# Placing the uses of one shared PSUM bank among the score tiles of an attention stage

## The reference, cut to what matters

```python
x = x + 0.5 * ffn(layernorm(x))        # 8 experts, top 2, and a shared one
x = x + attention(layernorm(x))        # 16 heads of 64, latents of 128
x = x + 0.5 * ffn(layernorm(x))        # x is (8, 1024, 256)

def attention(x):
    h = layernorm(x) * ln_scale + ln_bias
    c_q, c_kv = h @ w_down_q.T, h @ w_down_kv.T        # latents
    q, k, v = (c_q @ w_up_q.T, c_kv @ w_up_k.T, c_kv @ w_up_v.T)   # per head
    q, k = rope(q), rope(k)
    p = softmax(q @ k.T / 8)
    return (p @ v) @ w_out.T + x
```

## Time and profile before

| | |
|---|---|
| median of 3 runs | 4113.1 us (4110.75 to 4115.69) |
| profiled execution: its time | 4111.56 us |
| its span, first to last instruction | 4109.6 us |
| PE busy | 3897.7 us, 95% |
| POOL / DVE / ACT busy | 2948.8 / 2856.5 / 2535.5 us |
| mean granted TensorE clock | 0.987 |

### The profile page before, as it was taken

One profiled execution on the slowest core, in us unless ns is written; L12 is line 12 of the kernel. 1 busy time (PEld: TensorE's weight loads), 2 busy tenths in 40 slices (PEclk: granted clock), 3 DMA queues, 4 the chain that ended last, 5 costly groups with the idle time before them and its releaser, 6 DMA issues. The chain is left out here.

```text
span 4109.6 us, 65751 instructions
## 1 busy us (share of the span) xinstructions
PE 3897.7 (95%) x24908; PEld 2207.4 (54%) x24908; DVE 2856.5 (70%) x3794; ACT 2535.5 (62%) x3191; POOL 2948.8 (72%) x1634
## 2 busy tenths in 40 slices
PE   6999979999999999999999999999999999989999
PEld 6888844444444444444444444444444444478888
DVE  5565567777777776777778777767777777555563
ACT  4544437766766676667666766766676666545544
POOL 3444448878887887888788878878887888634444
PEclk9999989999999999999999999999999999999999
DMA  3332321111211221121112212211211122042331
GB/s 103 118 124 80 109 93 53 58 55 60 84 53 52 69 67 51 58 85 53 53 62 80 63 53 65 68 53 58 86 53 53 60 79 66 30 137 81 124 114 62
DMA packets 192771, 300.36 MB, mean 73 GB/s; under 512 B 50327, under 2 KB 100936, under 8 KB 191816
## 3 DMA queue, kind: packets, MB, share of 16 engines
q1 hardware_dynamic: 192456, 296.17, 22.3%
HBM read 201.20 MB, written 26.73 MB: 55 GB/s over the span
## 5 line engine op out<-in xcount | busy, mean ns | idle before, releaser
L1081 DVE TENSOR_REDUCE atNM<-atPS 128x2 f32<-128x1024 f32 x1024 | 1225.7, 1219 | 451.2 <-PE atPS L892 448.2
L1022 ACT ACTIVATE atPT<-atPS 128x1024 f32<-128x1024 f32 x1024 | 1013.9, 1024 | 773.5 <-PE atPS L913 766.8
L1180 POOL TENSOR_TENSOR atACC<-atACC,atPT 128x1024 f32<-128x1024 f32 x510 | 1238.4, 2428 | 89.6 <-ACT atPT L1022 39.4
L924 PE MATMUL atPO<-atPT,atV 128*64 128x512 f32 x4096 | 1014.1, 602 | 0.0
L1180 POOL TENSOR_TENSOR atACC<-atPT 128x1024 f32<-128x1024 f32 x255 | 606.5, 2378 | 259.4 <-PE atOT L946 180.8
L1013 ACT ACTIVATE atPS<-atSH 128x1024 f32<-128x1024 f32 x683 | 687.4, 1022 | 52.1 <-DVE atNM L1081 33.9
L913 PE MATMUL atPS<-atQH,atKL 64*128 64x512 f32 x2048 | 459.4, 445 | 67.4 <-DVE atPS L1087 53.0
L924 PEld LDWEIGHTS atPO<-atPT,atV 128*64 128x64 f32 x4096 | 258.9, 136 | 456.2 <-issue 432.9
L892 PE MATMUL atPS<-atKH,atQH 64*128 64x512 f32 x2048 | 443.7, 430 | 9.9 <-ACT atQH L1002 7.9
L1087 DVE COPY atPS<-atSH 128x1024 f32<-128x1024 f32 x341 | 418.7, 1228 | 38.6 <-DMA atSH<-atMD 11.8
L913 PE MATMUL atPS<-atQH,atKH 64*128 64x512 f32 x2048 | 405.9, 392 | 0.0
(11 more groups left out here) (278 smaller groups left out, 6480.4 us busy)
## 6 DMA issues: line engine op xcount, KB each, us to landing
atSH<-atMD SPq DMA_DIRECT2D x128, 512.0 KB, 4.3
atVT<-atR SPq DMA_DIRECT2D x508, 128.0 KB, 2.1
f1GB<-f1GD SPq DMA_DIRECT2D x128, 256.0 KB, 6.9
f2GB<-f2GD SPq DMA_DIRECT2D x128, 256.0 KB, 6.8
atRSUM<-atRD SPq DMA_DIRECT2D x126, 256.0 KB, 4.0
X<-x SPq DMA_DIRECT2D x4, 1024.0 KB, 5.7
XS<-x SPq DMA_DIRECT2D x16, 256.0 KB, 3.1
x<-X SPq DMA_DIRECT2D x16, 256.0 KB, 2.1
```

The lines of the kernel that those rows point to most:

```text
L924: ins = pe.eng.matmul(PO[HI[h], :], V[n % 2][:, j, HI[h]], PT[k % NPT][:, h, :], start=j == 0, stop=j == T - 1)
L1022: act.eng.activation(PT[k % NPT][:, :, :], PS[ring.of[step]][:, :, :], ACT.Exp, scale=SCALE).then_inc(grown.sem)
L1081: dve.eng.tensor_reduce(NM[:, q // 4, :, q % 4, t], PS[ring.of[step]][:, :, :], AX.X, ALU.max, negate=True).then_inc(most_out.sem)
L1180: pool.eng.tensor_tensor(total[:, :, :], begun[:, :, :], PT[k % NPT][:, :, :], ALU.add).then_inc(gathered.sem)
```

## The change

Three things change, all in the order of steps:

1. The first spot of a group now takes the steps of two ticks, `others_of(x)` and `others_of(x + 1)`; the second spot keeps those of `others_of(x + 2)` alone, now ahead of its attends.
2. If two or more steps of the shared bank come together in the first spot, a new function `apart` puts the raise among them behind the attends and gathers of that spot. Any others stay next to each other.
3. `TURNS` moves a batch's second two turns and its latents to other ticks.

No instruction is added or removed.

```diff
-            TURNS = [(-21, late), (-20, late), (-17, early), (-17, late), (-9, early), (-9, late), (-8, early), (-8, late)]
+            TURNS = [(-21, late), (-20, late), (-17, early), (-17, late), (-13, late), (-12, late), (-9, late), (-8, late)]
...
+            def apart(steps):
+
+                uses = [s for s in steps if s[0] in ("turn", "latent", "raise", "value", "row", "sum", "outward")]
+                if len(uses) < 2:
+                    return steps, []
+                return [s for s in steps if s[0] != "raise"], [s for s in steps if s[0] == "raise"]
...
-                order += others_of(x) + held + tile("attend", x - 1)
-                order += gathers(held + tile("attend", x - 1))
+                one, two = apart(others_of(x) + others_of(x + 1))
+                now = held + tile("attend", x - 1)
+                order += one + now + gathers(now) + two
...
-                order += tile("fill", x + 3) + others_of(x + 1) + tile("fill", x + 4) + now + gathers(now) + others_of(x + 2)
+                order += tile("fill", x + 3) + others_of(x + 2) + tile("fill", x + 4) + now + gathers(now)
```

## The result

The changed kernel takes 4302.0 us (median of 4 runs, 4296.2 to 4304.8) beside 4112.9 for the kernel before: ratio 1.046, 95% interval 1.044 to 1.048. It is slower, as forecast, but by 189 us where 70 were forecast, and it lies 76 us above the range.

What follows compares the result with a forecast made beforehand. The prediction took PE, busy for 95% of the span, as the bound. Its terms -82 + 114 + 12 + 26 = +70 us gave 4181.6 profiled, hence 4183 us; its own range was 4125 to 4215, a wider one 4115 to 4226.

Steps and rivals of the forecast that it cites:

- -82 us taken away: PE's waits in attention: 45 us of DVE-fill waits, 32 us of sums behind raises and 5 us more go.
- The sum no longer stands close behind a raise: 32 us go: Shared bank: PE's 32.0 us of waits, 23 times, for the second pass over a raise ahead of a sum disappear.
- +114 us, neighbours in one bank: Steps now adjacent in the shared bank make PE wait while it is emptied; 124 such pairs instead of 23.
- +12 us, one attend between: A raise moved by `apart` has one attend as cover: 5 us behind rows' copies, 7 us behind turns' copies.
- +26 us, DVE's maxima later: Raises in the first spot delay DVE's row maxima and so ACT's fill of tile x+3; half of 51 us taken.
- At no cost: DMAs of moved steps cost nothing: rows' leave earlier, raises' at most an attend later, and POOL has time to spare.
- by the trace they don't, and the sum has nothing for it: PE's clock: new standstills bring no swings, since the granted clock stayed at 1.00 despite standstills up to 2.3 us; 0 us.
- the rule: Skill page: frequent small idle times of PE between matmul groups, cycling through PSUM banks, can make its clock swing between levels.
- the rival's 136: PE's clock falls: one in twenty of 342 groups at 1.2 GHz, 136 us more, about 4320 us; chance 0.03.

Runs made afterwards that it cites:

- e11: Kernel before, with only the next tick's row brought up directly behind a value in the first spot: 4145.5 us, ratio 1.009.
- e6: Changed kernel, with `apart` leaving only the first use of the bank ahead of the first spot's attends, all others behind them: 4183.3 us, ratio 1.017.
- e7: Changed kernel, with raises of the second tick put at the end of the second spot, behind its attends: 4287.5 us, ratio 1.043.
- e9: Kernel before with new TURNS and only thin first spots filled; DVE and SP take brought-forward raises' passes and DMAs at their old place: 4082.0 us, ratio 0.993.
- e3: Changed kernel, with the step minus put ahead of the fill of tile x+2 in the first spot's group: 4259.8 us, ratio 1.037.
- e4: Changed kernel, with POOL's rotations of the raised tiles two ticks later: 4303.3 us, ratio 1.047.

## Why the prediction was wrong

By its own steps, each with what the changed profile shows. The first four, the missing one and 4 us of rows behind raises that no term had add up to +159 us beside the 157 by which PE's idle time grew; the clock comes on top.

- *"-82 us taken away"*: it was -52. The fill's part was right (53.0 to 9.4). The step that failed in this term is **"The sum no longer stands close behind a raise: 32 us go"**: 25.1 us stayed, 20 times. At the second place shown a score stands between the two on PE, but DVE comes to the raise's passes only behind the fill and the query subtraction. The timeline of the changed kernel, in a group of this kind (19 of the 20 waits are 1.04 to 1.22 us):

```profile
888.19 1.91 DVE L1084 TENSOR_TENSOR atQL<-atU,atQH 128x1024 fp32r<-128x1024 f32 x1
...
890.62 0.68 DVE L1073 TENSOR_TENSOR atU<-atOT,atCOS 128x512 f32<-128x512 f32 x1
...
891.36 1.06 PE L954 MATMUL atOT<-atACC,atones 128*32 128x512 f32 x8 [1.22 <-DVE atU L1073]
```

  I had counted PE's steps between raise and sum and not DVE's.
- *"+114 us, neighbours in one bank"*: the mechanism and the prices were right. Value, then row or sum, 29.9 + 24.6 us in 42 times (1.3 each, forecast 1.5); row, then value, 22.4 in 21 times (1.07, as from the earlier trace rows); outwards 0.79 as in the earlier trace rows, 14 more than before; some 13 behind ACT's other copies; in all about +104. e11 shows the pair of value and row by itself; for the other kinds the lengths stand in the changed kernel's list, and e6 took them away together.
- *"+12 us, one attend between"*: about +6 (7.8 for raises behind ACT's copies, of which 1.9 were there before). Behind a row's copy a raise waited once, 0.4 us in all, where 5 us were forecast; behind a turn's copy 3.5 in place of 7; two waits behind a sum's copy, 3.9 us, were not forecast.
- *"+26 us, DVE's maxima later"*: it was +59 (13.6 to 72.2). The mechanism was right (e7, e9); the size lay even above the upper end, 51, and I took half for no reason that a row gave. That DVE catches up in PE's standstills did not come true. **This term is 33 us too small.**
- **Missing: the row's own input.** The step counted whom the bank makes wait and not what the moved step itself needs. 38.0 us in 22 times; e3 shows it.
- *"At no cost"*, of the DMAs: right for the time (e4), though POOL's wait for the raises' DMAs rose from 50.0 to 390.8 us.
- **"by the trace they don't, and the sum has nothing for it"**, of the clock: PE's busy time grew by 32.5 us. The 1.00 of the earlier trace rows is a mean over 1000 us, in which a fall of a few us does not show. In stretches of 50 us from 600 to 3600 us, 2 of the 60 have a granted clock below 1.00 in the kernel before, and 11 in the changed one. The first of the two before the change, by the stretch of 50 us, one of 4 us and PE's timeline:

```profile
1300.00:1350.00 50.00, 48.10 (x318) 23.04 (x320) 36.41 (x43) 31.71 (x38) 38.17 (x21) 0.97 0.17 53
1302.00:1306.00 4.00, 4.00 (x21) 2.34 (x18) 1.40 (x2) 1.84 (x3) 3.39 (x2) 0.57 0.15 56
```

```profile
1301.37 1.09 PE L946 MATMUL atOT<-atACC,atones 128*32 128x512 f32 x8 [2.30 <-DVE atU L1065]
```

  So the clock had already fallen behind a single standstill of 2.30 us, of the very kind that the prediction names; the other fall (at 3425 us) stands behind one of 2.11 us. Three sums of the same kind (2.25, 2.08 and 2.14 us) had no fall behind them. The trace did not speak against the rule; I read it too coarsely. Stretches of the changed kernel, granted clock behind POOL's busy time:

```profile
2200.00:2205.00 5.00, 3.88 (x24) 1.46 (x22) 4.86 (x8) 2.72 (x4) 4.03 (x3) 1.00 0.19 57
2205.00:2209.00 4.00, 2.15 (x15) 1.10 (x16) 2.77 (x4) 3.28 (x4) 3.86 (x4) 1.00 0.02 2
2209.00:2213.00 4.00, 4.00 (x13) 1.18 (x12) 0.00 (x0) 0.27 (x1) 3.86 (x2) 0.57 0.44 126
```

  and what PE did there, from its timeline:

```profile
2204.86 0.50 PE L921 MATMUL atPS<-atQH,atKL 64*128 64x512 f32 x2 [1.12 <-ACT atPS L1021]
...
2208.80 0.27 PE L907 MATMUL atOT<-ident,atMC 128*8 128x128 f32 x1 [1.85 <-DVE atMC L1100]
2209.00 3.61 PE L932 MATMUL atPO<-atPT,atV 128*64 128x512 f32 x8
```

  Behind two standstills of 1.12 and 1.85 us the granted clock is 0.57 over 4 us, most of them at the lower level of 1.2 GHz, and the two attends took 3.61 us where the kernel before needs 1.94. In seven of the eleven stretches a row's wait for the maxima (1.84 to 1.86 us) comes just ahead of the fall, with 1.10 to 1.19 us of waiting for a fill some 4 us before. But the same two waits stand at five more places with no fall behind them, for instance here:

```profile
1002.47 0.27 PE L907 MATMUL atOT<-ident,atMC 128*8 128x128 f32 x1 [1.86 <-DVE atMC L1100]
```

```profile
1002.00:1006.00 4.00, 3.53 (x19) 1.37 (x21) 0.81 (x3) 0.27 (x1) 3.72 (x2) 1.00 0.33 98
```

  What decides between the two is not shown. What the rows do show is the number: from 600 to 3600 us the kernel before has 6 standstills of over 1.7 us with falls behind 2, the changed kernel 17 with falls behind 9, and e3, where the row's wait is mended, 6 with falls behind 5. The changed kernel has most of both, but the share is not fixed: e11 has 8 with a fall behind 1, and a few falls come behind shorter ones. The size: the stretches below 1.00 lose 20.5 us of full clock in the changed kernel (nine at 0.97, two at 0.93), 3.0 before and 9.5 in e3. So about 17 of the 32.5 us are the clock's by this measure, and 11 of the 17.9 that e3 won back; the rest of PE's longer busy time stays open.

  The rule that I had weighed and set at 3 in 100 (the Trainium skill, "TensorE: Matmul & The Clock Gate", section "A second HAM failure mode: psum-queue depth-cycling") holds here in its direction; its size is some 17 us and not the rival's 136. That the measured 4302 us lie near that rival's 4320 is chance: most of the loss is PE's idle time.

So the direction was right, and its largest term too. The size was missed by a wait that wasn't looked for (38), a term that was halved (33 too little), a wait wrongly taken as gone (25), and PE's longer busy time (32.5, some 17 of it by the clock), which the sum had at nothing.

Of the 59 us of late ACT fills, 36 went when the second tick's raises went (e7, 72.2 to 35.9). How the other 22 divide between query subtractions and other steps of DVE was not measured apart.

## What to carry to other kernels

A step that is moved up has to be checked against three things in every engine's order, not in PE's alone: who empties the buffer that it takes, what produces its own input, and what it is put ahead of on the engines that serve it. Filling one thin place with work from the next one pays only if the serving engine isn't the same for both; here 19 of 23 us came back at the next fill. Where the bound engine is busy for 95%, as here, a wait was paid in full (e11), and the clock may fall behind it on top. A mean over 1000 us cannot show that a clock never falls: look at short stretches just behind the longest standstills.

## What the runs showed of the hardware that was not expected

The granted clock of TensorE can fall for a few us in the middle of dense work, right behind a standstill of about 2 us: 0.57 of full over the 4 us behind a single wait of 2.30 us in the kernel before, whose PE is busy for 95%, and 0.57 over the 4 us behind waits of 1.12 and 1.85 us in the changed one. It need not fall: behind 3 of 5 such waits of 2.08 to 2.30 us in the kernel before, and behind 5 of 12 such pairs of waits in the changed one, it stayed at 1.00.
